# A graph attention kernel: probabilities doubly buffered, the output written by VectorE with its residual, another order in the slot and at the end

## The reference, cut to what matters

```python
    # --- layer 0 ---  A = adj @ h; C - A is the same for all i up to b, since both weights are adj
    h = jnp.maximum(_layernorm(x, axis=-1), 0.0)
    x = x + _L0_gnn_ref(h, adj, adj, L0_gnn_b)
    # --- layer 1 ---
    h = jnp.maximum(_layernorm(x, axis=-1), 0.0)
    x = x + _L1_gnn_ref(h, adj, Wq, bq, Wk, bk, Wv, bv)

def _L0_gnn_ref(x, W1, W2, b):
    A = jnp.einsum('od,bdn->bon', W1, x)
    C = jnp.einsum('od,bdn->bon', W2, x) + b[None, :, None]
    return jnp.max(jax.nn.relu(A[:, :, None, :] + (C - A)[:, :, :, None]), axis=-1)

def _L1_gnn_ref(x, adj, Wq, bq, Wk, bk, Wv, bv):       # 8 heads of 64
    q, k, v = x @ Wq + bq, x @ Wk + bk, x @ Wv + bv    # each split into heads
    scores = jnp.einsum('bihd,bjhd->bhij', q, k) / 8 + where(adj == 0, -1e9, 0)
    return jnp.einsum('bhij,bjhd->bihd', softmax(scores), v)
```

## Time and profile before

| | |
|---|---|
| median of 3 runs | 1403.61 us (1401.77 to 1403.91) |
| the profiled execution's own time | 1401.24 us |
| its span, first to last instruction | 1399.4 us |
| TensorE busy | 1310.5 us, 94% |
| GpSimd busy | 1251.0 us, 89% |
| VectorE busy | 1125.2 us, 80% |
| ScalarE busy | 878.7 us, 63% |
| granted TensorE clock | 1.00 from 50 to 1344 us, 0.86 before, 0.55 after |

### The profile page before, as it was taken

How to read it: one execution, slowest core, us unless ns; L and a number is a source line. 1 busy time by engine, 2 the same in 40 slices (tenths; PEclk the granted TensorE clock), 3 DMA queues, 4 the chain that set the end, 5 groups by cost and what they waited for, 6 DMA issues and landing times.

```text
span 1399.4 us, 32539 instructions
## 1 busy us (share of the span) xinstructions
PE 1310.5 (94%) x11145; PEld 657.2 (47%) x11145; DVE 1125.2 (80%) x1460; ACT 878.7 (63%) x1294; POOL 1251.0 (89%) x1288
## 2 busy tenths in 40 slices
PE   4899999999999999999999999999999999999962
PEld 1344444444444444454445444444444444444531
DVE  6468878888888788788898888888789888887874
ACT  4666666666666666666666666666666666666531
POOL 2889999999999999999999999999999999999721
PEclk8999999999999999999999999999999999999975
DMA  6235554555545545556455554655545556555534
GB/s 197 60 84 107 136 129 114 138 123 123 139 113 132 130 113 140 123 123 139 112 137 126 125 137 112 137 125 124 136 115 135 128 120 140 115 134 114 90 78 104
DMA packets 441372, 171.66 MB, mean 123 GB/s; under 512 B 406784, under 2 KB 406912, under 8 KB 441344
## 3 DMA queue, kind: packets, MB, share of 16 engines
q1 hardware_dynamic: 440000, 171.03, 52.7%
q10 hardware_dynamic: 1344, 0.27, 0.1%
HBM read 37.03 MB, written 33.55 MB: 50 GB/s over the span
## 4 chain that ended last, share of the span: by engine, by line
PE 55%; DMA 22%; DVE 15%; issue 4%; SPq 2%; ACT 1%; DVEq 0%; POOL 0%; POOLq 0%; ACTq 0%
PE proj L691 26%; DMA probsT<-probs 21%; PE proj L703 13%; PE o_ps L735 7%; DVE probs L495 7%; PE proj L676 6%; PE sc L720 4%; DVE attn L527 3%; SPq L239 2%; DVE a_max L481 1%; DVE out_scale L523 1%; DVE mean_var L474 1%; DVE inv_sum L521 1%; DMA x_in<-in_x 0%; SPq L219 0%
## 5 line engine op out<-in xcount | busy, mean ns | idle before, releaser
L691 PE MATMUL proj<-hT,w 128*128 128x512 f16 x3072 | 688.4, 381 | 11.5 <-DMA hT<-h 7.1
L691 PEld LDWEIGHTS proj<-hT,w 128*128 128x128 f16 x3072 | 291.0, 98 | 360.3 <-issue 16.8
L703 PE MATMUL proj<-w,hT 128*128 128x512 f16 x1536 | 352.4, 379 | 1.1 <-DVE w L579 1.1
L339 POOL TENSOR_TENSOR qkT<-qk,qkT 128x512 f16<-128x512 f32 x256 | 298.6, 1167 | 12.1 <-ACT qk L392 11.9
L407 ACT ACTIVATE probs<-shifted 128x1024 f16<-128x1024 f32 x128 | 135.3, 1057 | 193.7 <-DMA probsT<-probs 180.3
L390 ACT ACTIVATE qkT<-proj,bqk_up 128x512 f16<-128x512 f32 x256 | 173.4, 677 | 108.3 <-PE proj L691 108.3
L481 DVE TENSOR_REDUCE a_max<-proj 128x1 f32<-128x512 f32 x124 | 85.8, 692 | 191.5 <-PE proj L676 191.3
L327 POOL TENSOR_TENSOR xbv<-x_in,bv_rows 128x512 f32<-128x512 f32 x128 | 227.6, 1778 | 10.6 <-POOL y L318 2.2
L703 PEld LDWEIGHTS proj<-w,hT 128*128 128x128 f16 x1536 | 149.9, 98 | 181.6 <-DVE w L579 1.5
L511 DVE TENSOR_TENSOR shifted<-masked,row_max 128x1024 f32<-128x1024 f32 x128 | 210.7, 1646 | 13.4 <-ACT probs L409 9.1
L318 POOL TENSOR_TENSOR y<-attn,x 128x512 f32<-128x512 f32 x128 | 162.6, 1271 | 48.6 <-DVE attn L527 48.6
(11 more groups left out here) (61 smaller groups left out, 1125.2 us busy)
## 6 DMA issues: line engine op xcount, KB each, us to landing
x_in<-in_x SPq DMA_DIRECT2D x128, 256.0 KB, 2.9
out_x<-y SPq DMA_DIRECT2D x128, 256.0 KB, 2.2
hT<-h SPq DMA_TRANSPOSE x128, 3.1
probsT<-probs SPq DMA_TRANSPOSE x128, 4.4
w_raw<-in_L_gnn_Wq SPq DMA_DIRECT2D x1, 1024.0 KB, 9.0
w_raw<-in_L_gnn_Wv SPq DMA_DIRECT2D x1, 1024.0 KB, 11.3
w_raw<-in_L_gnn_Wk SPq DMA_DIRECT2D x1, 1024.0 KB, 13.4
bv_rows<-in_L_gnn_bv ACTq DMA_DIRECT2D x1, 256.0 KB, 6.7
```

Source lines behind the costliest of these rows:

```text
L339: pool.tensor_tensor(qk_place(k, u, 1), qk32[:, u % 2, :], qk_place(k, u, 0), ALU.subtract).then_inc(qk_rest_done, 1)
L691: last = nc.tensor.matmul(proj[:, u % 2, :], w16[:, j, s, c, col * P:(col + 1) * P], hT[:, k // GROUP % 2, t, c, :, :].rearrange("p g n -> ...
L703: last = nc.tensor.matmul(proj[:, V_BANK, :], hT[:, k // GROUP % 2, s, c, k % GROUP, :], w16[:, 2, t, c, :], start=(c == 0 and i == 0), st ...
```

## The change

- `probs16` and `probsT` get two buffers each, `probsT_done` becomes two semaphores. Exp now waits for the transpose of two graphs before, the transpose for the PV of two graphs before.
- SP's program is written out for all 128 slots, each DMA with its own waits, in the order load, transpose of h, store, transpose of the probabilities.
- `attn` and GpSimd's `finish` go. VectorE's attention_out writes y itself, a scalar_tensor_tensor for each of the eight heads: (o_ps x out_scale) + x1, 64 columns each. The release of `o_ps` to TensorE and the store now both follow y_done.
- VectorE's order becomes softmax of k-5, a_max of k+3, v_rest of k-1, moments of k+6, attention_out of k-7, aggregation, probs_rest of k-5. TensorE does PV last in the slot. GpSimd and ScalarE treat x1 and its column of graph k in slot k, not k-1.
- At the end three pairs of banks hold scores, the rests of the last five graphs' probabilities are made by GpSimd, and attention_out is two graphs behind the softmax.

```diff
-        probs16 = sb("probs16", [P, 2, H, P], F16)
-        probsT = sb("probsT", [P, 2, H, P], F16)
+        probs16 = sb("probs16", [P, 2, 2, H, P], F16)
+        probsT = sb("probsT", [P, 2, 2, H, P], F16)
-        attn = sb("attn", [P, 2, D])
-        pairs_of_banks = (sc, proj[:, 0:2, :])
+        TAIL_BANKS = (sc, proj[:, 0:2, :], proj[:, 2:4, :])
...
             def transpose(base, k):
                 if in_range(base, k):
+                    m = base + k
+                    sp.wait_ge(h_rest_done, m + 1)
+                    wait(sp, qk_ready, 2 * (m - m % GROUP - GROUP))
+                    wait(sp, v_ready, m + 1 - 2 * GROUP)
...
             def transpose_probs(base, k):
                 if in_range(base, k):
-                    sp.dma_start_transpose(probsT[:, :, :, :]...
+                    sp.wait_ge(probs_rest_done, base + k + 1)
+                    wait(sp, o_ready, base + k - 1)
+                    sp.dma_start_transpose(probsT[:, k % 2, :, :, :]...
...
             def slot(base, k):            # SP
-                if isinstance(base, int):
-                    load(base, k + LOAD_AHEAD)
-                else:
-                    sp.wait_ge(o_evac, base + k - OUT_BEHIND + 1)
-                    sp.dma_start(x_in[:, k % RING, :], x[base + k + LOAD_AHEAD, :, :])...
-                if isinstance(base, int) and in_range(base, k - ATTN_BEHIND):
-                    sp.wait_ge(probs_rest_done, base + k - ATTN_BEHIND + 1)
-                    wait(sp, o_ready, base + k - ATTN_BEHIND)
-                transpose_probs(base, k - ATTN_BEHIND)
...
+                load(base, k + LOAD_AHEAD)
                 transpose(base, k + TURN_AHEAD)
                 store(base, k - STORE_BEHIND)
+                transpose_probs(base, k - ATTN_BEHIND)
-            slots(sp, slot)
+            for k in range(B):
+                slot(0, k)
...
-            def finish(base, k):          # GpSimd: y = attn + x1
...
+            def probs_rest(base, k):      # GpSimd, the last five graphs only
+                    pool.tensor_tensor(probs16[:, k % 2, 1, :, :], probs[:, :, :], probs16[:, k % 2, 0, :, :],
+                                       ALU.subtract).then_inc(probs_rest_done, 1)
             def slot(base, k):            # GpSimd
-                add_c(base, k + X1_AHEAD)
+                add_c(base, k)
                 rest(base, k + NORM_AHEAD)
                 qk_rest(base, k, u)
                 norm_scales(base, k + MOMENTS_AHEAD)
                 qk_rest(base, k, u + 1)
-                finish(base, k - OUT_BEHIND)
...
-                    wait(act, probsT_done, m * 16)
+                    wait(act, probsT_done[k % 2], (m - k % 2) * 8)
...
             def attention_out(base, k):   # VectorE
-                    if in_range(base, k + OUT_BEHIND + NORM_AHEAD):
-                        dve.wait_ge(h_rest_done, m + OUT_BEHIND + NORM_AHEAD + 1)
 ...
-                    wait(dve, y_done, m - 1)
-                    nc.vector.tensor_tensor(attn[...], o_view[...], out_scale[...], ALU.mult).then_inc(o_evac, 1)
+                    dve.wait_ge(x1_done, m + 1)
+                    wait(dve, y_stored[k % 2], (m - k % 2) * 8)
+                    for h in range(H):
+                        cols = slice(h * HD, h * HD + HD)
+                        last = nc.vector.scalar_tensor_tensor(y[:, k % 2, cols], o_view[:, h // 4, h % 4, 0:HD],
+                                                              out_scale[:, h // 4, h % 4:h % 4 + 1],
+                                                              x1[:, k % RING, cols], ALU.mult, ALU.add)
+                    last.then_inc(y_done, 1)
...
             def slot(base, k):            # VectorE
                 softmax_shift(base, k - ATTN_BEHIND)
-                v_rest(base, k - 1)
+                if not isinstance(base, int) or base + k > 0:
+                    adjacency_out(base, k + AMAX_AHEAD)
+                v_rest(base, k - V_BEHIND)
                 stats_of(base, k + MOMENTS_AHEAD)
                 moments_wait(base, k + MOMENTS_AHEAD)
-                adjacency_out(base, k + PREP_AHEAD)
+                attention_out(base, k - Y_BEHIND)
                 moments_of(base, k + MOMENTS_AHEAD)
                 probs_rest(base, k - ATTN_BEHIND)
-                attention_out(base, k - OUT_BEHIND)
-            softmax_shift(*TAIL[0], pairs_of_banks[0])
-            for i, (base, k) in enumerate(TAIL):
-                if i + 1 < len(TAIL):
-                    softmax_shift(*TAIL[i + 1], pairs_of_banks[(i + 1) % 2])
-                probs_rest(base, k)
-                attention_out(base, k - 1)
-            attention_out(*TAIL[-1])
+            for i, graph in enumerate(TAIL):
+                softmax_shift(*graph, TAIL_BANKS[i % 3])
+                attention_out(B, graph[1] - Y_BEHIND + ATTN_BEHIND)
+            for k in range(-Y_BEHIND + ATTN_BEHIND, 0):
+                attention_out(B, k)
...
             def probs_times_v(base, k):   # TensorE
-                    pe.wait_ge(probsT_done, (m + 1) * 16)
+                    pe.wait_ge(probsT_done[k % 2], (m - k % 2) * 8 + 16)
                     pe.wait_ge(v_evac, m + 1)
-                    wait(pe, o_evac, m)
+                    wait(pe, y_done, m)
             def slot(base, k):            # TensorE
                 qk_chunk(base, k, u + 1)
-                probs_times_v(base, k - OUT_BEHIND)
                 adjacency(base, k + PREP_AHEAD)
                 v_rows(base, k)
+                probs_times_v(base, k - OUT_BEHIND)
```

More of the change, by code:

```diff
@@ L154, in graph_layers @@
             sem("s_ready"), sem("masked_done"), sem("max_done"), sem("shifted_done"), sem("probs_done"))
-        probs_head_done, probs_rest_done, probsT_done = sem("probs_head_done"), sem("probs_rest_done"), sem("probsT_done")
-        o_ready, inv_sum_done, out_scale_done, o_evac = sem("o_ready"), sem("inv_sum_done"), sem("out_scale_done"), sem("o_evac")
-        c_done, xc_done, x1_done, y_done = sem("c_done"), sem("xc_done"), sem("x1_done"), sem("y_done")
+        probs_head_done, probs_rest_done = sem("probs_head_done"), sem("probs_rest_done")
+        probsT_done = [sem(f"probsT_done{i}") for i in range(2)]
+        o_ready, inv_sum_done, out_scale_done, y_done = sem("o_ready"), sem("inv_sum_done"), sem("out_scale_done"), sem("y_done")
+        c_done, xc_done, x1_done = sem("c_done"), sem("xc_done"), sem("x1_done")
         def wait(eng, s, count):
@@ L309, in rest @@
                                        ALU.subtract).then_inc(h_rest_done, 1)
-            def finish(base, k):
[L313 to L318, removed]
-                                       ALU.add).then_inc(y_done, 1)
             def add_c(base, k):
@@ L348, in _ @@
             pool.wait_ge(bias_loaded, 64)
-            for k in range(X1_AHEAD):
-                add_c(0, k)
             assert (NORM_AHEAD, MOMENTS_AHEAD) == (5, 6)
@@ L359, in slot @@
                 qk_rest(base, k, u + 1)
-                finish(base, k - OUT_BEHIND)
             slots(pool, slot)
-            for k in range(-OUT_BEHIND, 0):
-                finish(B, k)
+            for graph in TAIL:
+                probs_rest(*graph)
         @block.scalar
@@ L405, in exps @@
                     act.wait_ge(shifted_done, m + 1)
-                    wait(act, probsT_done, m * 16)
-                    nc.scalar.activation(probs16[:, 0, :, :], shifted[:, :, :], ACT.Exp, scale=HD ** -0.5).then_inc(probs_head_done, 1)
+                    wait(act, probsT_done[k % 2], (m - k % 2) * 8)
+                    nc.scalar.activation(probs16[:, k % 2, 0, :, :], shifted[:, :, :], ACT.Exp, scale=HD ** -0.5).then_inc(probs_head_done, 1)
                     wait(act, probs_rest_done, m)
@@ L440, in _ @@
             act.wait_ge(bias_loaded, 64)
-            for k in range(X1_AHEAD):
-                c_of(0, k)
             def slot(base, k):
@@ L480, in adjacency_out @@
                     wait(dve, c_done, m - RING + 1)
-                    nc.vector.tensor_reduce(a_max[:, k % RING, :], proj[:, A_BANK, :], AX.X, ALU.max).then_inc(a_evac, 1)
+                    rows = FIRST_BANKS[k] if isinstance(base, int) and m < PREP_AHEAD else proj[:, A_BANK, :]
+                    nc.vector.tensor_reduce(a_max[:, k % RING, :], rows, AX.X, ALU.max).then_inc(a_evac, 1)
             def v_rest(base, k):
@@ L494, in probs_rest @@
                     dve.wait_ge(probs_done, base + k + 1)
-                    nc.vector.tensor_tensor(probs16[:, 1, :, :], probs[:, :, :], probs16[:, 0, :, :],
+                    nc.vector.tensor_tensor(probs16[:, k % 2, 1, :, :], probs[:, :, :], probs16[:, k % 2, 0, :, :],
                                             ALU.subtract).then_inc(probs_rest_done, 1)
@@ L587, in first_rest @@
                 nc.vector.tensor_tensor(h16[:, k, 1, :], h32[:, k % 2, :], h16[:, k, 0, :], ALU.subtract).then_inc(h_rest_done, 1)
-            def first_adjacency_out(k):
-                dve.wait_ge(a_ready, k + 1)
```

(13 more changed lines are left out.)

33 lines of the change are left out of this document (12 added, 21 removed).

## The result

The changed kernel takes 1435.72 us (median, 1434.3 to 1436.96) against 1403.61 (1401.77 to 1403.91): 1.0231 of the time before, 95% interval 1.0214 to 1.0249. It is slower by 32 us, where 43 us less were forecast.

What follows compares the result with a forecast made beforehand. TensorE needs 10.03 us a slot; PV's waits for late transposed probabilities lose 36.3 us in the middle. -36.3 + 6 (hold-ups) - 12.6 (end) + 0.2 (start) = -42.7, so 1403.6 becomes 1361 us; range 1352 to 1387.

Steps and rivals of the forecast that it cites:

- y from 6.91 (0.50 for reciprocal and scale: 604.61 to 605.11): VectorE's new order: y starts 6.91 us after the slot's scores, reciprocal and scale taking 0.50, read from the old trace.
- the ring: Closed chain of waits through TensorE and VectorE (scores, softmax, y, PV, next scores): 9.37 us long, under TensorE's 10.03.
- The port that VectorE and GpSimd share: Part on VectorE's shifted against GpSimd's xbv and x1: whichever starts first holds the other; 0.05 us per slot put down.
- the 6 us for other hold-ups: Allowance in the middle for held-up shifted and y's additional register wait: 0.05 us per slot, 6 us in all.
- The transpose on time: Transpose of the probabilities lands near 4.6 of the next slot, PV wants it at 9.30: 4.7 us to spare.
- SP's new order harmless: SP's queue: load, transpose of h and store wait for nothing later than probs_rest, so the order holds nothing up.
- p = 0.20: Spacing in us of VectorE's eight y instructions per slot: eight are 1.6, the last ends 1.68 after the first starts.
- Slower: Rival, 8%: the eight y instructions don't overlap, 0.28 us apart; slot 10.52, 1416 us.
- L: Hold-up of VectorE's shifted by GpSimd in a slot: forecast 0, or 0.5 us if xbv holds it.
- The narrow gap: VectorE's shifted, at 3.46, falls between GpSimd's xbv ending 3.44 and x1 beginning 3.59, so it is not held.
- The end: Last slot's scores to the last y's end: 49.9 us instead of 62.5, gain 12.6, with three bank pairs.
- The start: First slots: slot 1's adjacency product waits for an a_max behind w_rest, 0.2 us once.

Runs made afterwards that it cites:

- number 1: Changed kernel with the reciprocal's result (inv_sum) in unused columns of o_ps in PSUM, so out_scale no longer reads SBUF: 1356.18 us, ratio 0.9667.
- number 7: Changed kernel without the scale instruction (V's column of ones set to 1/undo), the last graph's rest on VectorE: 1360.03 us, ratio 0.9701.
- number 5: Kernel before with only two buffers for probs16 and probsT and SP's new order and waits; both engines' old orders, attn and old end kept: 1378.45 us, ratio 0.9824.
- number 8: Kernel before with double buffers and SP's new order, y per head on VectorE and inv_sum in PSUM, both engines' old orders: 1356.37 us, ratio 0.9677.
- number 2: Kernel before with inv_sum in PSUM and nothing else: 1402.18 us beside 1401.95, ratio 1.0004.
- number 9: As number 8 (double buffers, old orders, y per head on VectorE), but with the reciprocal's result back in SBUF: 1360.92 us, ratio 0.9697.
- 11: As number 8 (double buffers, old orders, y per head on VectorE), but without the scale instruction, V's ones column holding 1/undo: 1353.64 us, ratio 0.9647.
- number 10: Changed kernel with the reciprocal's result in PSUM and the rest of the last graph's probabilities on VectorE instead of GpSimd: 1354.99 us, ratio 0.9658.
- number 3: Changed kernel with GpSimd's first rest of q/k doing half its columns in the loop's 112 slots: 1381.14 us, ratio 0.985.

## Why the prediction was wrong

**The step that failed** is "y from 6.91 (0.50 for reciprocal and scale: 604.61 to 605.11)". The duration was read where GpSimd ran only inv_std beside it, and moved into an order where GpSimd begins its second rest of q/k at that time. It measured 1.37. In number 1, with nothing held, the same piece is 0.61 in the slot shown and 0.57 on average, so some 0.8 us is the hold-up and the rest belongs to the piece itself. The other pieces of the ring were short by 0.42 together, none by more than 0.12; without the hold-up they stay hidden (9.37 + 0.42 = 9.79, under TensorE's 10.03; number 1 has slots of 10.03 with some 0.2 us to spare), and with it the ring is 10.66 and 117 slots pay for it. The part "The port that VectorE and GpSimd share" asked the right question of shifted alone ("whichever of these tensor_tensors starts first holds the other") and never of the other VectorE instructions on the path, where the longest duration of each group would have shown it: 932 ns for out_scale in the kernel before. Priced at 0.85 by itself it would have given 9.37 + 0.85 = 10.22 a slot, 14 us saved in the middle and 1377 (1383 with the 6 us for other hold-ups); that the change loses took the 0.42 as well.

The Trainium skill states it too: "SBUF — State Buffer", in SBUF: two separate sides, has the shared pair of ports as an exclusive lock for a whole instruction, taken on VectorE's side by instructions in a two-port mode, or with two SBUF inputs where GpSimd's instruction reads SBUF, and "VectorE: DVE Perf Modes" (Mode 2×_2P) puts tensor_scalar with a source in SBUF in that mode and rules it out for PSUM. The runs agree with both beside the rest of q/k: 1.08 us with the source in SBUF, 0.226 with it in PSUM. They differ from the first beside inv_std: by an exclusive lock the scale begun 0.03 after it would have waited for its end, and it took 0.23 and ended 0.29 before it (by GpSimd's spans, which are rough in the profile). The measurement decides: not every GpSimd instruction holds it. That the eight columns run in the two-port mode was not measured by itself.

**Point by point.**
- The transpose on time, no wait of PV for probsT, SP's new order harmless: right. SP's wait for the probabilities is 57.3 us in 75 slots and holds nothing that is due.
- p = 0.20: right. Eight pieces are 1.62 to 1.63, 276 ns each, so they start 0.19 apart and overlap by 0.08. The rival "Slower" was right that the change would lose, but it put its slow slot, 10.52, on pieces that do not overlap, and they do; the slots came out at 10.72 for another reason.
- L and the hold-ups of shifted: small in the middle of the changed kernel (0.13 in the slot shown). The narrow gap was real: number 7 fell into it.
- The end: 49.9 forecast, 50.2 measured, GpSimd's rest 2.3 forecast, 2.13 measured. The size is right, the credit is not: number 5 has as short an end without the bank pairs, since the second buffer ends exp's wait for the transfer. Once VectorE writes y, the old end is somewhat longer, 54.5 to the end of the span in number 8 against 52.6 in number 1 (these two differ in the order as well), so the new end may be worth up to 2 us there; it was not run by itself.
- The start: +1.35, not +0.2. The runs can't tell this from nothing: the control, number 2, reaches its first slot of the middle at 98.83, 2.3 later than the kernel before, and takes the same time.
- With the one cause out, number 1, the change gives 1356.2, 5 below the forecast of 1361: of the 6 us put down for hold-ups its middle needed 1.3 (1174.8 against 117 x 10.03).

**The order.** By numbers 8, 9 and 11 VectorE's and TensorE's new orders bring nothing: the old orders give 10.03 a slot as well, once y has left GpSimd and the probabilities have two buffers. What the new order did was take VectorE's slack of 1.12 us a slot out of the ring. That the scale meets the rest of q/k is not its doing alone: number 5 has the meeting in the old order, with y on GpSimd, and does not have it any more in number 9, with y on VectorE.

## What to carry to other kernels

When VectorE's order is changed, lay GpSimd's instructions beside it in the new order and price every VectorE instruction that meets one with what it takes when it is held: here a 128x8 one went from 0.23 to 1.08 us. A group's maximum in the kernel before tells which instructions were held at least once, so read it beside the median. Keep a small result that VectorE will read again in PSUM if a free column is at hand, or fold its factor in elsewhere; and lay the two engines beside each other again after each such edit, since taking the scale out cost 5 us in the new order (number 7 against number 10). Before believing an account of a gain, run the cheapest part alone: two buffers by themselves made the end as short as the whole change did.

## What the runs showed of the hardware

- A tensor_scalar of 8 columns, SBUF to SBUF, that starts beside a GpSimd tensor_tensor of 512 columns (256 in number 3) ends 0.02 to 0.04 after it: 1.08 us beside 1.15, 0.42 beside the rest of 0.67. Beside the 128x1 inv_std of 0.55 it takes 0.23 and is not held. With its source in PSUM it takes 0.226 beside the rest of q/k. The reciprocal that reads PSUM and writes SBUF is not held either: 0.20 at 1324.57 in the kernel before, with the rest of q/k begun at 1324.55.
- It goes the other way as well: GpSimd's var_eps, 128x1, begun at 612.15 in the changed kernel, takes 1.08 beside VectorE's probs_rest (611.99, 1.19) and ends 0.05 after it; the shortest of the 128 takes 0.189.
- Eight scalar_tensor_tensor of 64 columns with a pointer scalar and a source in PSUM take 1.62 us together and 0.276 each, so they start 0.19 apart and one starts 0.08 before the last one's end.
